# Last stage of a graph network: one sweep for column sums and squares, own rows scaled by ScalarE

## The reference, cut to what matters

```python
msg = x[src] * alpha[:, :, None]                 # edges, and one loop edge for each node
out = jax.ops.segment_sum(msg, dst, num_segments=n)
h = out.reshape(n, H * C) + bias
mu = jnp.mean(h, axis=0)                         # for each column, over all 6250 nodes
var = jnp.var(h, axis=0)
h = (h - mu) * jax.lax.rsqrt(var + BN_EPS) * gamma + beta
h = jax.nn.elu(h)
return feature + h
```

## Time and profile before

| | us |
|---|---|
| median of three runs | 4758.05 |
| lowest and highest | 4743.52, 4765.12 |
| profiled execution | 4761.29 |
| its span, first to last instruction | 4758.8 |
| first gather of the last stage starts at | 4527.71 |
| mean granted TensorE clock | 0.797 of full |

### The profile page before, as it was taken

How to read it: one execution, slowest core, us unless ns; L and a number is a source line. 1 busy time by engine, 2 the same in 40 slices (tenths; PEclk the granted TensorE clock), 3 DMA queues, 4 the chain that set the end, 5 groups by cost and what they waited for, 6 DMA issues and landing times. The chain is left out here.

```text
span 4758.8 us, 56459 instructions
## 1 busy us (share of the span) xinstructions
PE 2853.5 (60%) x10779; PEld 1822.5 (38%) x10780; DVE 3061.9 (64%) x6090; ACT 1481.4 (31%) x3656; POOL 2084.0 (44%) x2102
## 2 busy tenths in 40 slices
PE   0799997666666674000177776766355666556632
PEld 0455554433334342000155554434244444445421
DVE  5333334555555554999899998676366666666665
ACT  0122223333333332231033333434234433434302
POOL 1000005777777774000033333222577777777550
PEclk9999998777877777555599999899677777777765
DMA  4344447999999997000155554000466666666531
GB/s 154 111 137 137 140 140 253 315 312 316 315 314 315 314 315 247 0 0 0 66 197 200 201 196 151 15 18 17 108 188 193 191 185 191 192 189 193 158 122 54
DMA packets 648045, 815.90 MB, mean 171 GB/s; under 512 B 155094, under 2 KB 552310, under 8 KB 647602
## 3 DMA queue, kind: packets, MB, share of 16 engines
q1 hardware_dynamic: 532228, 457.32, 30.0%
q0 software_dynamic: 115696, 357.28, 24.7%
HBM read 541.33 MB, written 274.25 MB: 171 GB/s over the span
## 5 line engine op out<-in xcount | busy, mean ns | idle before, releaser
L821 POOL DMA_INDIRECT rows<-kv,kvi x880 | 832.7, 946 | 890.9 <-DVEq L893 623.0
L1721 POOL DMA_INDIRECT g_rows<-x1t,srci x880 | 848.8, 965 | 286.3 <-issue 259.4
L866 PE MATMUL psD<-qs,hot 128*128 x1760 | 702.9, 525 | 247.7 <-DVE prod L907 193.3
L907 DVE TENSOR_TENSOR prod<-rows,psD 128x256 f32<-128x256 f32 x880 | 363.6, 417 | 465.4 <-DMA rows<-kv,kvi 353.9
L1875 PE MATMUL g_psM<-g_rows,g_hot 128*128 128x264 f32 x1760 | 570.8, 479 | 77.5 <-DVE g_rows L1993 71.0
L1157 POOL TENSOR_TENSOR wv<-vrows,wgt 128x1024 f32<-128x1024 f32 x110 | 219.5, 1996 | 840.0 <-DMA vrows<-val_v 622.3
L866 PEld LDWEIGHTS psD<-qs,hot 128*128 128x128 f32 x1760 | 381.6, 252 | 521.0 <-issue 309.6
L1237 PE MATMUL psM<-wv,vhot 128*128 128x260 f32 x1760 | 445.7, 397 | 138.4 <-DVE run L1256 131.5
L1875 PEld LDWEIGHTS g_psM<-g_rows,g_hot 128*128 128x128 f32 x1760 | 390.0, 233 | 171.9 <-issue 94.2
L1237 PEld LDWEIGHTS psM<-wv,vhot 128*128 128x128 f32 x1760 | 318.1, 190 | 265.9 <-DVE run L1256 219.3
L886 ACT ACTIVATE off<-psB,npiota 128x256 f32<-128x256 f32 x440 | 207.7, 472 | 669.8 <-PE psB L857 667.8
(11 more groups left out here) (359 smaller groups left out, 4634.8 us busy)
## 6 DMA issues: line engine op xcount, KB each, us to landing
val_v<-rows SPq DMA_DIRECT2D x220, 512.0 KB, 5.0
vrows<-val_v SPq DMA_DIRECT2D x220, 512.0 KB
kv<-stage SPq DMA_DIRECT2D x98, 768.0 KB, 4.7
sums_v<-g_run SPq DMA_DIRECT2D x110, 528.0 KB, 3.6
g_drow<-drow_v SPq DMA_DIRECT2D x55, 512.0 KB
rows<-kv,kvi POOLq DMA_INDIRECT x880, 5.0
g_rows<-x1t,srci POOLq DMA_INDIRECT x880
g_ndt<-nodeb SPq DMA_DIRECT2D x440, 6.0 KB
```

The costliest lines, as they stand in the source:

```text
L821: nc.gpsimd.indirect_dma_start(out=rows[:, k], out_offset=None, in_=table, in_offset=bass.IndirectOffsetOnAxis(ap=index[:, i * SLOTS + k:i ...
L866: nc.tensor.matmul(psD[:, k % 4, 0:cols], hot[:, t % 2, j * P:(j + 1) * P], node[:, ds(blk[t], 1)].rearrange("p o d -> p (o d)"), start=Tr ...
L907: ins = nc.vector.tensor_tensor(prod[:, k % 4], rows[:, k, 0:D], psD[:, k % 4, 0:D], ALU.mult)
L1721: nc.gpsimd.indirect_dma_start(out=rows[:, i % NBUF, k, 0:ROW1], out_offset=None, in_=dr["x1t"], in_offset=bass.IndirectOffsetOnAxis(ap=v[ ...
```

## The change

The bias is no longer added to the rows: it is added to the mean. The rows are centred about a provisional mean, the column mean of the first group alone, formed by PE in a third PSUM bank and by DVE in `start`. So sums and squares of the centred rows can be taken group by group in the first pass; the variance is the mean square less the squared mean of the centred rows.

ACT multiplies own rows by their weight, in 28 activations of 128x64 for each group (`own_rows`), and squares the group before. `xw`, `t1` and `sq` have two buffers. DVE handles weights and scaling of group b + 1 before it completes group b. PE sums group b and then its squares. The first x load goes ahead of the vectors, the second waits for nothing.

In the last pass, `shift` holds beta, less 1, less the centred mean times `gain`. DVE makes `y` (normalised value less 1), then `max(y, -1) + x`, then adds `min(exp(y + 1), 1)`; ACT's exponential adds the 1. `y` and `ex` have two buffers; loops are written out. GpSimd's part is as before.

Of the lines removed only four are shown; the rest stands in the code above.

```diff
...
-xw = sb("fxw", [P, G7, D])
...
+xw = sb("fxw", [P, 2, G7, D])
+own = sb("fown", [P, NB, H])
...
+t1 = sb("ft1", [P, 2, G7, D])
...
-sq = sb("fsq", [P, G7, D])
...
+sq = sb("fsq", [P, 2, G7, D])
+y = sb("fy", [P, 2, G7, D])
+ex = sb("fex", [P, 2, G7, D])
+psS = tmp.enter_context(nc.psum_tensor("psS", [P, 3, 512], F32))
...
     def _(sp):
+        def load(b):
+            if b >= 2:
+                sp.wait_ge(t1_done, b - 1)
+            sp.dma_start(xw[:, b % 2], dr["x1t"][b * G7 * P:(b + 1) * G7 * P, 0:D].rearrange("(k p) d -> p k d", p=P)).then_inc(x_in[b % 2], 16)
+        load(0)
...
+        for b in range(1, NG7):
+            load(b)
+        for b in range(NG7 - 1):
             sp.wait_ge(o_done, b + 1)
...
+            sp.dma_start(out[b * G7 * P:(b + 1) * G7 * P, :].rearrange("(k p) d -> p k d", p=P), xs[:, group(b)]).then_inc(saved, 16)
...
     def _(act):
...
+        def own_rows(b):
+            act.wait_ge(own_w, b + 1)
+            act.wait_ge(x_in[b % 2], 16 * (b // 2 + 1))
+            if b >= 2:
+                act.wait_ge(h_done, b - 1)
+            for k in range(G7):
+                for h in range(H):
+                    ins = nc.scalar.activation(t1[:, b % 2, k, h * DK:(h + 1) * DK], xw[:, b % 2, k, h * DK:(h + 1) * DK],
+                                               ACT.Copy, scale=own[:, b * G7 + k, h:h + 1])
+            ins.then_inc(t1_done, 1)
+        def squares(b):
+            act.wait_ge(mid, b + 1)
+            if b >= 2:
+                act.wait_ge(sq_sum, b - 1)
+            nc.scalar.activation(sq[:, b % 2], acc[:, group(b), 0:D], ACT.Square).then_inc(sq_done, 1)
+        for b in range(NG7):
+            own_rows(b)
+            if b >= 1:
+                squares(b - 1)
+        squares(NG7 - 1)
+        act.wait_ge(root_in, 1)
+        nc.scalar.activation(gain[:], gain[:], ACT.Sqrt, bias=c["eps"][:, 0:1]).then_inc(root, 1)
+        for b in range(NG7):
             act.wait_ge(y_done, b + 1)
...
+            if b >= 2:
+                act.wait_ge(o_done, b - 1)
+            nc.scalar.activation(ex[:, b % 2], y[:, b % 2], ACT.Exp, bias=1.0).then_inc(ex_done, 1)
...
     def _(pe):
...
+        def column_sum(bank, source, b, start, stop):
+            for k in range(G7):
+                n = count(b, k)
+                ins = nc.tensor.matmul(psS[:, bank, 0:D], c["ones"][0:n], source(k, n),
+                                       start=start and k == 0, stop=stop and k == G7 - 1, skip_group_check=True)
+            return ins
+        pe.wait_ge(h_done, 1)
+        column_sum(2, lambda k, n: acc[0:n, k, 0:D], 0, True, True).then_inc(start_sum, 1)
+        def both(b):
+            pe.wait_ge(mid, b + 1)
+            column_sum(0, lambda k, n: acc[0:n, b * G7 + k, 0:D], b, b == 0, b == NG7 - 1).then_inc(sums, 1)
+            pe.wait_ge(sq_done, b + 1)
+            column_sum(1, lambda k, n: sq[0:n, b % 2, k], b, b == 0, b == NG7 - 1).then_inc(sq_sum, 1)
+        for b in range(NG7):
+            both(b)
...
     def _(dve):
...
+        def weights(b):
+            mine, dn, lo = acc[:, group(b), D + H:MSG], den[:, group(b)], low[:, group(b)]
+            dve.wait_ge(acc_in[b], 16 * G7)
+            step(tt(dn, acc[:, group(b), D:D + H], mine, ALU.add))
+            step(tsc(lo, dn, 0.5, None, ALU.is_lt))
+            step(tt(mine, mine, lo, ALU.add))
+            step(tt(dn, dn, lo, ALU.add))
+            step(nc.vector.reciprocal(dn, dn))
+            tt(own[:, group(b)], mine, dn, ALU.mult).then_inc(own_w, 1)
+            dve.wait_ge(own_w, b + 1)
+        def scaled(b):
+            r = rows(b).rearrange("p k (h d) -> p k h d", h=H)
+            step(tt(r, r, of_head(den, b), ALU.mult))
+        def whole(b):
+            dve.wait_ge(t1_done, b + 1)
+            tt(rows(b), rows(b), t1[:, b % 2], ALU.add).then_inc(h_done, 1)
+            dve.wait_ge(h_done, b + 1)
+        def around(b):
+            tt(rows(b), rows(b), every(start[:]), ALU.subtract).then_inc(mid, 1)
+        weights(0)
+        scaled(0)
+        whole(0)
+        weights(1)
+        scaled(1)
+        dve.wait_ge(start_sum, 1)
+        step(tsc(start[:], psS[:, 2, 0:D], 1.0 / (G7 * P), None, ALU.mult))
+        around(0)
+        for b in range(1, NG7):
+            if b + 1 < NG7:
+                weights(b + 1)
+                scaled(b + 1)
+            whole(b)
+            around(b)
+        dve.wait_ge(w_in, 48)
+        dve.wait_ge(sums, NG7)
+        step(tsc(col[:], psS[:, 0, 0:D], 1.0 / N, None, ALU.mult))
+        step(tt(start[:], start[:], vec[:, 0], ALU.add))
+        step(tt(mean[:], start[:], col[:], ALU.add))
+        step(tt(shift[:], start[:], mean[:], ALU.subtract))
+        step(tt(col[:], col[:], col[:], ALU.mult))
+        dve.wait_ge(sq_sum, NG7)
+        stt(out=gain[:], in0=psS[:, 1, 0:D], scalar=1.0 / N, in1=col[:], op0=ALU.mult, op1=ALU.subtract).then_inc(root_in, 1)
+        dve.wait_ge(root, 1)
+        step(nc.vector.reciprocal(gain[:], gain[:]))
+        step(tt(gain[:], gain[:], vec[:, 1], ALU.mult))
+        step(tt(shift[:], shift[:], gain[:], ALU.mult))
+        stt(out=shift[:], in0=shift[:], scalar=-1.0, in1=vec[:, 2], op0=ALU.add, op1=ALU.add).then_inc(ready, 1)
+        dve.wait_ge(ready, 1)
+        def normed(b):
+            step(tt(rows(b), rows(b), every(gain[:]), ALU.mult))
+            if b >= 2:
+                dve.wait_ge(ex_done, b - 1)
+            tt(y[:, b % 2], rows(b), every(shift[:]), ALU.add).then_inc(y_done, 1)
+            dve.wait_ge(y_done, b + 1)
+            x_ = xs[:, group(b)]
+            step(stt(out=x_, in0=y[:, b % 2], scalar=-1.0, in1=x_, op0=ALU.max, op1=ALU.add))
+        def result(b):
+            dve.wait_ge(ex_done, b + 1)
+            x_ = xs[:, group(b)]
+            stt(out=x_, in0=ex[:, b % 2], scalar=1.0, in1=x_, op0=ALU.min, op1=ALU.add).then_inc(o_done, 1)
         for b in range(NG7):
...
-            stp(tt(heads(t1[:]), heads(xw[:]), of_head(zero, b), ALU.mult), 1)
...
-            tt(rows, rows, every(vec[:, 0]), ALU.add).then_inc(f_done, 1)
...
+            normed(b)
+            result(b)
```

More of the change, by code:

```diff
@@ L2119, in _ @@
+                for b in range(NG7):
                     act.wait_ge(y_done, b + 1)
-                    nc.scalar.activation(neg[:], neg[:], ACT.Exp).then_inc(e_done, 1)
+                    if b >= 2:
+                        act.wait_ge(o_done, b - 1)
+                    nc.scalar.activation(ex[:, b % 2], y[:, b % 2], ACT.Exp, bias=1.0).then_inc(ex_done, 1)
             @block.tensor
             def _(pe):
[L2125 to L2137, removed]
@@ L2145, in _ @@
                 tt, tsc, stt = nc.vector.tensor_tensor, nc.vector.tensor_scalar, nc.vector.scalar_tensor_tensor
[L2146 to L2150, removed]
                 def of_head(ap, b):
-                    return ap[:, ts(b, G7)].unsqueeze(3).to_broadcast([P, G7, H, DK])
+                    return ap[:, group(b)].unsqueeze(3).to_broadcast([P, G7, H, DK])
@@ L2155, in every @@
                 def every(ap):
                     return ap.unsqueeze(1).to_broadcast([P, G7, D])
-                for b in range(NG7):
[L2158 to L2172, removed]
-                    stp(tt(heads(t1[:]), heads(xw[:]), of_head(zero, b), ALU.mult), 1)
-                    dve.sem_inc(x_used, 1)
-                    stp(tt(heads(rows), heads(rows), of_head(den, b), ALU.mult), 2)
-                    stp(tt(rows, rows, t1[:], ALU.add), 3)
-                    tt(rows, rows, every(vec[:, 0]), ALU.add).then_inc(f_done, 1)
@@ L2178, in _ @@
[L2178 to L2186, removed]
@@ L2187, in _, with rows @@
-                step(nc.vector.reciprocal(g_[:], g_[:]))
-                step(tt(g_[:], g_[:], vec[:, 1], ALU.mult))
-                dve.wait_ge(d_done, NG7)
-                with dve.Fori(0, NG7) as b:
-                    def stq(ins, n):
-                        ins.then_inc(st4, 1)
-                        dve.wait_ge(st4, b * 3 + n)
-                    rows = acc[:, ts(b, G7), 0:D]
-                    x_ = xs[:, ts(b, G7)]
-                    stq(tt(rows, rows, every(g_[:]), ALU.mult), 1)
-                    stq(tt(pos[:], rows, every(vec[:, 2]), ALU.add), 2)
-                    tsc(neg[:], pos[:], 0.0, None, ALU.min).then_inc(y_done, 1)
-                    stq(stt(out=pos[:], in0=pos[:], scalar=0.0, in1=x_, op0=ALU.max, op1=ALU.add), 3)
-                    dve.wait_ge(e_done, b + 1)
-                    stt(out=x_, in0=neg[:], scalar=-1.0, in1=pos[:], op0=ALU.add, op1=ALU.add).then_inc(o_done, 1)
-                    dve.wait_ge(o_done, b + 1)
+                def rows(b):
+                    return acc[:, group(b), 0:D]
```

32 lines of the change are left out of this document (13 added, 19 removed).

## The result

The changed kernel took **4701.4 us** in the median (4696.98 to 4708.23), beside 4759.4 for the kernel before: a ratio of 0.9878, 95% interval 0.9864 to 0.9893, which is 58 us less (51 to 65). On another chip it came to 0.9867 (0.9847 to 0.9887), 63 us. The forecast was 4699, 59 us less.

The account below looks back on a forecast made before the run. POOL's gathers, stretched by DVE, were taken as the first bound, then DVE, ACT and PE in turns, then DVE in the sweep. Savings of 6.2 + 43.4 + 9.7 = 59.3 us from the 4758.05 median gave 4699, range 4688 to 4712.

Parts of the forecast that it names:

- Gathers up to T: First pass, 49 gathers on POOL: fewer full-width DVE operations leave 16.4 us of stretch, 6.2 us saved, bounds 0 to 8.
- T: Start of the last group's weights on DVE, 4613.08 before the change and forecast at 4606.9.
- the even picture of three in every group: First pass: three full-width DVE operations hold up gathers in each later group, making a group's time 11.6 us.
- ScalarE's new work: Own rows on ACT: 28 activations of 0.24 us, 6.8 us a group, hidden in mid-stream but not at the end.
- The tail: After the last weights: four queued PE sums take 15.6 us and end at T + 23.3; 43.4 us saved until the sweep.
- the first sum: First of PE's last four column sums: 5.7 us as the clock rises, then 3.3 us for each later one.
- Statistics: Between PE's last sum and the last sweep's first product: 4.1 us, the mean's operations hidden under the last square sum.
- The last sweep: Final DVE pass: 8.28 us a group instead of 9.67, 9.7 us saved, bounds 7 to 10.5.
- the wait for two events: Last sweep: DVE's first fused operation was priced at 2.13 us because it waits for two events.
- Rival 1: PE's column sums: PE keeps the lower clock, gain 55 us (4703) or 40 us (4718); chance 0.24.
- Rival 2: First-pass gathers: POOL's stretch does not shrink, gain 53 us, 4705; chance 0.12.
- Rivals 3 and 4: Own rows on ACT: ACT sets the pace, at 0.586 us apiece 4743 (chance 0.04), at 0.85 slower, 4794 (0.02).

## Why the prediction was right, step by step

**Gathers up to T.** Forecast 6.2 us, measured 5.5 in one profile and, against the same row of before, 8.4 in the other, just past the upper bound of 8. POOL's first gather and the last three of the changed kernel:

```profile
4529.66 0.94 POOL L2100 DMA_INDIRECT facc<-sums_v,lastvisit  x1 [33.06 <-POOLq L69]
...
4600.99 2.67 POOL L2100 DMA_INDIRECT facc<-sums_v,lastvisit  x1 [0.30 <-issue]
4603.97 1.75 POOL L2100 DMA_INDIRECT facc<-sums_v,lastvisit  x1 [0.30 <-issue]
4606.02 1.75 POOL L2100 DMA_INDIRECT facc<-sums_v,lastvisit  x1 [0.30 <-issue]
```

Three long ones where the earlier trace rows has four. The count that the forecast rests on is right, 16 long gathers where before has 24, one for each full-width operation that meets them; the even picture of three in every group is not: the seven groups have 0, 1, 2, 4, 2, 4 and 3, and their weights start 8.4 to 15.4 us apart, not 11.6. That costs nothing up to T, because POOL never pauses for longer than 0.30 us. The stretch is 4606.02 + 1.75 - 4529.66 - 60.95 = 17.2 us (forecast 16.4). That a gather is held up by an operation with two SBUF tensors was inferred from the earlier trace rows and is now shown by taking the operands away: 17.2 (14.2 in the other profile), 5.0 and 0.0 us of stretch with three, one and no such operation a group. In the Trainium skill, "SBUF — State Buffer", section "SBUF: two separate sides", VectorE and GpSimd share one pair of ports that either holds for a whole instruction, VectorE when it reads two SBUF inputs while the GpSimd instruction reads SBUF too. The traces agree in so far as a gather is held until 0.8 us after such an operation's end and never beside one with an operand in PSUM; which port holds it no run here shows.

**ScalarE's new work.** Forecast 0.24 us apart, 6.8 a group, hidden in mid-stream, 0.7 us of wait at the end. The group of own rows (shapes, count | busy us, mean ns | idle before):

```profile
L2132 ACT ACTIVATE ft<-fxw,fown 128x64 f32<-128x64 f32 x196 | 47.5, 334 | 45.0 <-DVE fown L2195 45.0
```

47.5/7 = 6.79 us, and the wait for the last group was 0.69 (below). No table load came in.

**The tail.** Forecast: PE starts at T + 7.65 and needs 15.6 us, end at T + 23.3. The timeline from T on, with an earlier sum ahead of it:

```profile
4560.89 4.97 PE L2159 MATMUL psS<-facc,ones 128*128 128x256 f32 x14 [2.65 <-DVE facc L2208]
...
4609.51 0.19 DVE L2190 TENSOR_TENSOR fden<-facc 128x28 f32<-128x28 f32 x1 [2.56 <-DMA facc<-sums_v,lastvisit]
...
4610.98 6.80 ACT L2132 ACTIVATE ft<-fxw,fown 128x64 f32<-128x64 f32 x28 [1.78 <-DVE fown L2195]
...
4612.73 3.19 PE L2159 MATMUL psS<-fsq,ones 128*128 128x256 f32 x14
...
4617.17 3.29 PE L2159 MATMUL psS<-facc,ones 128*128 128x256 f32 x14 [1.26 <-DVE facc L2208]
...
4617.81 2.03 DVE L2204 TENSOR_TENSOR facc<-facc,ft 128x1792 f32<-128x1792 f32 x1 [0.69 <-ACT ft L2132]
4619.87 2.02 DVE L2208 TENSOR_TENSOR facc<-facc,fstart 128x1792 f32<-128x1792 f32 x1
...
4626.35 3.19 PE L2159 MATMUL psS<-fsq,ones 128*128 128x256 f32 x14
...
4633.81 2.03 DVE L2240 TENSOR_TENSOR facc<-facc,fgain 128x1792 f32<-128x1792 f32 x1
```

PE's last four sums begin at 4617.17, which is T + 7.66, and end at 4629.55, T + 20.0. **The term that was mis-sized is the first sum**: taken at 5.7 us, as a burst after an idle time, it took 3.29 (the other three came 3.0 us apart, not 3.3; together that makes 3.2). PE had summed the squares of group 4 until 4615.9 at the upper level, paused 1.26 us, and kept it:

```profile
4607.01:4612.70 5.69, 5.69 (x14) 0.54 0.10 25
4617.17:4629.54 12.37, 12.36 (x56) 1.00 0.00 1
```

The burst that began at 4607.01 after 8.29 us of idle time started low (0.54 on average, 5.69 us), as forecast for such a case. The prediction had named both sums of group 4, but took no account of how short they leave PE's pause. By its own numbers the pause was 2.6 us (11.6 - 5.7 - 3.3), and after 2.65 us a sum of this same profile took 4.97 (4560.89). The pause was 1.26 because the last groups' weights started only 10.2 us apart. In the version without two SBUF tensors a sum after a pause of 1.96 us took 4.98 (4601.26), while another of that profile after a pause of the same length took 3.29 (4592.99). So a pause of this length can go either way, and that the last sums kept the upper level was in part luck.

**Statistics.** Forecast 4.1 us from the last sum to the first product, measured 4633.81 - 4629.55 = 4.26. The five operations on the mean did lie under the last sum.

**The last sweep.** Forecast 8.28 us a group and 9.7 saved, measured 8.12 and 10.8:

```profile
4637.93 1.70 ACT L2152 ACTIVATE fex<-fy 128x1792 f32<-128x1792 f32 x1 [6.01 <-DVE fy L2243]
4637.93 2.02 DVE L2246 SCALAR_TENSOR_TENSOR xs<-fy,xs 128x1792 f32<-128x1792 f32 x1
4639.99 2.02 DVE L2251 SCALAR_TENSOR_TENSOR xs<-fex,xs 128x1792 f32<-128x1792 f32 x1
4641.94 2.02 DVE L2240 TENSOR_TENSOR facc<-facc,fgain 128x1792 f32<-128x1792 f32 x1
```

ACT's exponential (1.70) ends before the first fused operation does, so the wait for two events (2.13 in the forecast; its two rows are 2.15 apart) never came: 2.06. And the next product starts 1.95 us after the last fused operation, not 2.03, because VectorE no longer waits for its own result. Both small terms erred on the same side.

**Sum and rivals.** 5.5, 46.5 and 10.8, in all 62.9, against 6.2 + 43.4 + 9.7 = 59.3. The stage gained 3.6 us more than forecast (6.5 in the other profile), above all in the tail. That the median nevertheless lies within 3 us of 4699 is partly luck: the runs of either kernel spread over 11 to 22 us, and the last stage began 2 us later in the changed kernel's profile. Rival 1 (PE at the lower clock) didn't occur; the two rows of the second buffer's experiment show why. Rival 2 (no shorter stretch) fell. Rivals 3 and 4 have their mechanism confirmed by the doubled activations and their price refuted: 0.243 us apiece, not 0.586 or more.

Not tried: the bias on the mean by itself. In this kernel it saves no operation on VectorE, since the subtraction of the starting mean takes its place in the first pass and the old second pass is what goes.

## What to carry to other kernels

An engine that looks free may be the cheap one because of whom it doesn't disturb: if a full-width VectorE operation reads two SBUF tensors beside gathers, price it at its own time plus what it adds to the one gather that it holds up (on average 0.9 to 1.1 us here), and try one operand in PSUM before moving work away. When engines take turns through one tile, count both the turns and the slower clock that the pauses bring: a second buffer alone gave 26 of the 63 us. And once a pace-setter is made faster, look at the next one's slack before adding up the gain: here ScalarE, without a pause, took 8.27 us a group (4584.57 to 4592.84) against the gathers' 8.75, and that was too little to make up for a late start.

## What was not expected of the hardware

VectorE's 128x1792 operations take 2.02 us whether operands or result lie in SBUF or PSUM. GpSimd's subtraction of the same shape takes 3.97 to 3.99 us, twice VectorE's, and VectorE's operations with one PSUM operand keep their 2.02 us beside it; no run shows it alone. Each VectorE operation with two SBUF tensors holds up one gather, until 0.8 us after its own end. The stretch of the gathers differed by 3 us (17.2 and 14.2) between two executions of one kernel.
